# A dilation split over five engines: which taps go to GpSimd, DMA and PSUM chains

## Time and profile before

| | us |
|---|---|
| median of 3 runs | 10762.84 (10760.06 to 10778.29) |
| the profiled execution | 10759.57 |
| its span on the core | 10757.7 |
| mean granted TensorE clock of it | 0.965 |

### The profile page before, as it was taken

How to read it: one execution, slowest core, us unless ns; L and a number is a source line. 1 busy time by engine, 2 the same in 40 slices (tenths; PEclk the granted TensorE clock), 3 DMA queues, 4 the chain that set the end, 5 groups by cost and what they waited for, 6 DMA issues and landing times. The chain is left out here.

```text
span 10757.7 us, 72949 instructions
## 1 busy us (share of the span) xinstructions
PE 8270.0 (77%) x17056; PEld 3131.6 (29%) x17056; DVE 10336.3 (96%) x5749; ACT 9666.7 (90%) x6995; POOL 9024.2 (84%) x2890
## 2 busy tenths in 40 slices
PE   1777777777777777777777777777777777887888
PEld 0222222222222222222222222222222223333333
DVE  7999999999999999999999999999999998998999
ACT  2999999999999999999999999999999996776666
POOL 2888888888888888988888888888888885666898
PEclk9999999999999999999999999999999998998999
DMA  7777666676767677677666767667767764343666
GB/s 299 138 139 138 136 133 133 135 136 135 137 135 138 136 138 139 134 139 139 136 137 136 139 137 138 136 134 139 139 137 137 138 119 140 153 160 156 249 254 247
DMA packets 408034, 1618.63 MB, mean 150 GB/s; under 512 B 21920, under 2 KB 128416, under 8 KB 358048
## 3 DMA queue, kind: packets, MB, share of 16 engines
q0 software_dynamic: 243712, 971.69, 50.8%
q1 hardware_dynamic: 163872, 642.05, 16.1%
HBM read 397.22 MB, written 201.33 MB: 56 GB/s over the span
## 5 line engine op out<-in xcount | busy, mean ns | idle before, releaser
L482 POOL TENSOR_TENSOR m<-m,u 128x2048 f32<-128x2048 f32 x1536 | 6567.5, 4405 | 509.0 <-ACT m L576 507.7
L678 DVE SCALAR_TENSOR_TENSOR acc_a<-m,kt,acc_a 128x2048 f32<-128x2048 f32 x1472 | 3466.4, 2355 | 48.9 <-POOL m L482 3.4
L544 PE MATMUL chain<-dx,mats 128*128 128x512 f32 x6144 | 2950.4, 614 | 520.6 <-ACT chain L594 520.0
L544 PE MATMUL chain<-dx,neg_ident 128*128 128x512 f32 x4608 | 2325.6, 644 | 867.8 <-ACT chain L594 867.7
L678 DVE SCALAR_TENSOR_TENSOR acc_a<-t,kt,acc_a 128x2048 f32<-128x2048 f32 x896 | 2108.9, 2354 | 22.8
L544 PE MATMUL chain<-u,mats 128*128 128x512 f32 x3072 | 1570.2, 635 | 561.2 <-ACT chain L594 560.8
L576 ACT ACTIVATE m<-dx,gap_l 128x2048 f32<-128x2048 f32 x960 | 1921.5, 2002 | 59.2 <-POOL dx L444 34.3
L544 PEld LDWEIGHTS chain<-dx,mats 128*128 128x128 f32 x6144 | 1094.8, 191 | 2397.7 <-ACT chain L594 1387.3
L678 DVE SCALAR_TENSOR_TENSOR acc_a<-u,kt,acc_a 128x2048 f32<-128x2048 f32 x704 | 1655.9, 2352 | 13.7
L594 ACT ACTIVATE chain<-chain,gap_r 128x1024 f32<-128x1024 f32 x1536 | 1626.2, 1088 | 46.1 <-PE chain L544 40.0
L453 POOL DMA_DIRECT2D t<-u x896 | 1235.6, 1448 | 469.8 <-ACT t L576 464.0
(11 more groups left out here) (144 smaller groups left out, 6543.0 us busy)
## 6 DMA issues: line engine op xcount, KB each, us to landing
t<-u POOLq DMA_DIRECT2D x896, 1059.0 KB, 8.7
u<-x_dram SPq DMA_DIRECT2D x32, 2688.0 KB, 24.9
xw<-x_scratch SPq DMA_DIRECT2D x65, 1152.0 KB, 7.3
hw<-h_scratch SPq DMA_DIRECT2D x66, 1024.0 KB, 9.3
xt<-x_dram SPq DMA_DIRECT2D x32, 2048.0 KB, 14.4
x_scratch<-x SPq DMA_DIRECT2D x64, 1024.0 KB, 4.0
h_scratch<-h SPq DMA_DIRECT2D x32, 2048.0 KB, 7.3
out_dram<-res SPq DMA_DIRECT2D x64, 1024.0 KB, 4.9
```

Source lines behind the costliest of these rows:

```text
L482: nc.gpsimd.tensor_tensor(m[j % MP][:], m[j % MP][:], rows, ALU.add).then_inc(m_ready, 1)
L544: added = nc.tensor.matmul(chain[h][:, r:r + 2, :], weight, src[:, top:top + 2, dj:dj + W], start=False, stop=True, skip_group_check=True)
L678: nc.vector.scalar_tensor_tensor(out=acc_a[:], in0=src, scalar=k_base, in1=acc_a[:], op0=ALU.subtract, op1=ALU.max).then_inc(a_done, 1)
```

## The change

It moves taps between the four ways and reorders all four lists. Counted per chunk:

| | before | after |
|---|---|---|
| GpSimd pairs | 24 | 22, six of them clamped (pairs 1, 5, 9, 12, 16, 20) |
| DMA pairs | 14 | 16 |
| singles merged into `acc_a` | 11 | 9 |
| relus into m / into t | 24 / 14 | 16 / 16 |
| chains, left and right | 3 and 3 | 1 and 5 |
| half-steps of chains in each half (adds in PSUM) | 27 | 29 |

The rows of m get a pitch of 260 columns instead of 256, so they no longer join into one run of 2048. The clamp takes a minimum first and then a maximum on both sides. The two turns for differences are letters 21 and 35 of 46 in GpSimd's order; they were letters 11 and 24 of 40.

```diff
-CHAINS = ((0, "left"), (1, "left"), (2, "left"), (3, "right"), (4, "right"), (5, "right"))
-NPOOL, NDMA = 24, 14
-
-CLAMPED = ()
+CHAINS = ((0, "left"), (1, "right"), (2, "right"), (3, "right"), (4, "right"), (5, "right"))
+NPOOL, NDMA = 16, 16
+
+CLAMPED = (1, 5, 9, 12, 16, 20)
 MP, TP = 4, 4
...
-ACT_ORDER = "r0x1r01rx01b0r1x0r10r10u10x1r0r10rx10r1r0x1r0x10x10r10r10xr1r0r1x01r01x0r01xx10r0r10x10r10r1r1"
-PE_ORDER = "010101010101010101010101010101010101010100110010101011"
-DVE_ORDER = "mm0s1sysmmy0s1mmymsmm0y1msymmymy0s1smsmymymm0my1ymssym0ym1ymm"
-POOL_ORDER = "tittitittidtttitittiittditttiittititittt"
+ACT_ORDER = "x0x01r01xr10b1r01r01x01x01r01xr0u10r10x10x10x1r01r01r01x01x01x01r01r01x01r01rx010r10x10r10x1"
+PE_ORDER = "0011010101010101010101010101010101010101010101010101010101"
+DVE_ORDER = "m01mmymysss0m1myysymmy01mmsmyyms01msymsymm01ymymyysm0m1mymy"
+POOL_ORDER = "iitcitttcitittittcitdititcittiicttditittictitt"
...
-        m = [sb(f"m{s}", [P, CR, W]) for s in range(MP)]
+
+        m = [sb(f"m{s}", [P, CR, W + 4])[:, :, 0:W] for s in range(MP)]
...
-                    first, second = (ALU.max, ALU.min) if right else (ALU.min, ALU.max)
+                    gap = gap_l[:, g, at_col:at_col + 1]
+                    low, high = (gap, FAR) if right else (-FAR, gap)
 
                     pool.wait_ge(a_done, a_free(c, "m", j, NPAIR, MP))
                     passed(pool, pool_turns)
-                    nc.gpsimd.tensor_scalar(m[j % MP][:], dx[s][:, top:top + CR, lo:lo + W],
-                                            gap_l[:, g, at_col:at_col + 1], FAR if right else -FAR,
-                                            first, second).then_inc(m_clamped, 1)
+                    nc.gpsimd.tensor_scalar(m[j % MP], dx[s][:, top:top + CR, lo:lo + W], high, low,
+                                            ALU.min, ALU.max).then_inc(m_clamped, 1)
```

More of the change, by code:

```diff
@@ L477, in pair @@
                         pool.wait_ge(m_clamped, c * len(CLAMPED) + (CLAMPED.index(j) + 1))
-                        nc.gpsimd.tensor_tensor(m[j % MP][:], rows, m[j % MP][:],
+                        nc.gpsimd.tensor_tensor(m[j % MP], rows, m[j % MP],
                                                 ALU.add if outer > base else ALU.subtract).then_inc(m_ready, 1)
@@ L481, in pair @@
                         pool.wait_ge(m_begun, c * NRELU + (relu_pairs.index(j) + 1))
-                        nc.gpsimd.tensor_tensor(m[j % MP][:], m[j % MP][:], rows, ALU.add).then_inc(m_ready, 1)
+                        nc.gpsimd.tensor_tensor(m[j % MP], m[j % MP], rows, ALU.add).then_inc(m_ready, 1)
                 def chunk(c, s, k, w, ahead, loads):
@@ L613, in _ @@
                                         act.wait_ge(a_done, a_free(c, "m", relu_pairs[j], NPAIR, MP))
-                                        pair_relu(s, k, pool_pairs[relu_pairs[j]], m[relu_pairs[j] % MP][:]) \
+                                        pair_relu(s, k, pool_pairs[relu_pairs[j]], m[relu_pairs[j] % MP]) \
                                             .then_inc(m_begun, 1)
@@ L660, in merge @@
                             base = outer
-                        src = m[j % MP][:]
+                        src = m[j % MP]
                     elif kind == "y":
```

## The result

The changed kernel takes 10604.1 us (median of 4 runs, 10601.96 to 10607.43) beside 10767.14 us before; the ratio is 0.985 with a 95% interval of 0.9838 to 0.9863. The forecast was 10488 within 10400 to 10640. So it is faster, by 1.5%, and in the range, but 116 us of the 275 us that I expected to save did not come. The profiled execution took 10607.43 us, its span is 10605.6.

What follows compares the result with a forecast made beforehand. VectorE was taken to bound the dilation: floor 130.8 plus 1.3 us of waits makes 132.1 instead of 136.40 us a chunk, 275 us less over 64 chunks; 10759.6 - 275 + 3.3 = 10488 us, range 10400 to 10640.

Steps and rivals of the forecast that it cites:

- sign of being wrong: VectorE idle before m or before chain merges above some 200 us, or add at 4.15 us and clamp above 2.6.
- VectorE's floor, 130.8 us: VectorE's merge list per dilation chunk without waits: 135.09 - 4.78 + 0.5 us; floor as summed had chance 0.69.
- The waits: VectorE's waits per dilation chunk, put at 1.3 us like today's 1.31, where TensorE's clock falls; ends 0 and 3.
- hidden: Accumulating DMAs, 16 instead of 14 a chunk: queues at most 0.83 busy, 33 us per t buffer, no VectorE wait.
- seven tight places instead of two: Half-chains of relu, TensorE step and merge with at most 1.2 to 1.4 us slack: seven of twelve, before two.
- GpSimd's add, 3.6 us: GpSimd's add into m falls from 4.15 to 3.6 us because pitch 260 puts both inputs in rows.
- the other explanation: GpSimd's dh and dd take 3.6 us because they read one tensor twice, one element apart, not because of rows.
- The clamp, 2.7 us: GpSimd's one-input clamp of an m tile, six a chunk: 2.7 us each, between 1.8 and 4.54.
- the starving rival: GpSimd's list of 131 to 136 us a chunk half starves VectorE: 10609, reaching to 10750 us; chance 0.14.
- Later differences at no cost: GpSimd's later differences end its 2.2 us waits for u, gaining nothing; a window's last piece is ready 12 us early.
- The page's floor for two inputs: Trainium skill's about 2.5 cycles per element for GpSimd, 4497 ns per add; by it m's add could not fall.
- the rival that leaned on them: GpSimd becomes the bound: adds stay 4.15 us, clamp costs 4.15, list 140.1 us a chunk, 11000 us; chance 0.09.

## Why the prediction was right, and where it was off

The direction and the bound were right: VectorE paced the dilation before and after, and the two merges it lost are the gain. Neither sign of being wrong came up: VectorE idled 151.8 us before m merges in the dilation, the 14 gaps among them, and 65.6 before chain merges, each under 200, and the clamp stayed under 2.6 us. That the total fell into the range is in part luck, since the term for the waits came out at its very end.

- *VectorE's floor, 130.8 us*: right. 133.93 less the waits of 2.97 is 130.96, and 130.84 was seen. Two chain merges in a row start 1.19 us apart, so a pair costs the 0.12 us extra that I took.
- *The waits, "I take 1.3 us, with 0 and 3 as ends"*: this is the term that was mis-sized, 2.97 us. The upper end that I gave for it was summed wrong as well: 130.8 + 3 = 133.8 us a chunk makes 166 us less and about 10597, not 10610, and the measured time lies above that. The profiled execution missed its forecast by 10607.4 - 10484.6 = 122.8 us. Of these 1.67 x 64 = 107 are waits, 10 the floor (0.16 us a chunk), and 9.7 a later first merge (228.3 instead of 218.6); the part behind the dilation was 3.5 us shorter. The step under it failed in its reading: the 1.31 us of before were put down to TensorE's clock and the chains. A third of it was the fetch after a branch, behind GpSimd's name in the earlier trace rows, and I did not ask why it came 14 times, once a turn of the loop, or what DMAs placed in front of it would do to it. I had written the DMA off as "hidden".
- *The chains, seven tight places instead of two* (I count six on doing it again): right in kind for the place. Before, the waits stand at four of the twelve merges, after at eight, mostly smaller. For the size, "stay" holds about: 0.73 and 1.19 us a chunk in the two main traces, but 1.1 and 1.2 where both kernels ran on one chip.
- *GpSimd's add, 3.6 us*: wrong, 4.14. Rows and mixed forms were the wrong pattern to see in six rows of a profile in which layout and identity of the inputs change together. I had named the other explanation and given it too little. The error did not reach the time, since GpSimd was not the bound.
- *The clamp, 2.7 us*: 1.95, inside its bounds. 22 x 0.54 more and 6 x 0.75 less leave 7 us more on the list, 126 of 133, so GpSimd was no bound, but had no room at the edges: 0.64 us a chunk of the starving rival, in a kernel where no list is over its floor. The 1.24 us that I took for a DMA issue was a remainder of busy time; from start to start, with nothing to wait for, an issue takes 0.78 us in both traces, and by these distances the list is an estimated 22 x 4.14 + 16 x 0.78 + 2 x 1.91 + 6 x 1.94 = 119 us. So neither sum shows this wait: it comes from the order at the chunk's edges.
- *ScalarE and TensorE*: 124.6 and 112.6 us, as summed.
- *Later differences at no cost, GpSimd's wait for u gone*: right; the only wait of GpSimd for u left lies before the dilation's first chunk.
- *The page's floor for two inputs*: the Trainium skill, GPSIMD Engine Reference, section 3.1, gives 4497 ns for the add; the 2.5 cycles an element stand in its section 2.1. For m the rival that leaned on them came closer than my value. As a floor it does not hold: 3602 ns was measured on the same size.

## What to carry to other kernels

When one engine is at 98%, sum its list for the floor, and then treat the waits as terms of their own: how often each comes and at which place of the loop tells its cause better than the releaser's name. A loop's branch costs an instruction fetch that queues behind bulk DMA under way. On the engine that sets the pace, write the loop out, and then see in the trace which instruction carries which wait. An engine that is busy for 95% of the chunk can still starve another where two of its items stand in the wrong order: moving two DMA issues by a few places gave 0.5%. And before a small rise of a wait is put down to an edit, compare the two kernels on one chip.

## What the runs showed of the hardware

- From a taken branch to VectorE's next instruction: 3.3 to 4.3 us before, with one accumulating DMA under way that lands 2.1 to 3.1 us after the branch; 6.8 to 7.0 after, where it lands 6.5 to 6.7 us after; 2.8 to 3.2 with half the data, where none from before is left. The branch not taken: 0.09 us.
- GpSimd's two-input instruction on 128 x 2048 float32: 3.60 us for one tensor read one element apart, 3.81 one row apart, 4.17 in place, 4.52 for two tensors; with both inputs flat 4.49 in place. Its clamp: 1.97 us with the minimum first, 7.15 with the maximum first.
- TensorE, half the columns in each step: busy 60% instead of 84% of the time between 1000 and 8000 us, with a granted clock of 0.79 instead of 0.96.
- VectorE: a merge whose wait for the merge before stands in a separate instruction begins 0.07 us later.
